# The order in which SyncE stores keys and queries and loads the last context, at the passage into cross attention

## The reference

```
x = x + attn1(layernorm(x))                      # one head, causal
q = (layernorm(x) @ Wq.T + bq), k = (ctx @ Wk.T + bk), v = (ctx @ Wv.T + bv)   # 16 heads of 8
scores = q k^T / sqrt(8), masked with -1e9; p = softmax(scores)
x = x + (p v) @ Wo.T + bo
x = x + ffn(layernorm(x))                        # quantised, 384 hidden
```

## Time and profile before

| | |
|---|---|
| median of 3 runs | 327.62 us (327.48 to 327.71) |
| the profiled execution | 325.96 us |
| its span, first to last instruction | 324.2 us |
| granted TensorE clock, mean | 0.994 |

### The profile page before, as it was taken

The page is one execution under the profiler, slowest core; times in us unless marked ns, Lnnn a source line. Parts: engine busy times, 40 slices in busy tenths (PEclk is TensorE's granted clock), DMA queues, the critical chain, the costliest instruction groups (busy, mean ns, idle before and its releaser), DMA issues.

```text
span 324.2 us, 10009 instructions
## 1 busy us (share of the span) xinstructions
PE 300.0 (93%) x3765; PEld 206.9 (64%) x3765; DVE 271.4 (84%) x653; ACT 255.3 (79%) x470; POOL 193.0 (60%) x340
## 2 busy tenths in 40 slices
PE   6999999997999999999999999899978689699996
PEld 5787877786656666666666666844323244359996
DVE  5489988787889989999999975877789996899764
ACT  3578888985889998989999987797797758994930
POOL 3679999981338796967749578200077773784000
PEclk9999999999999999999999999999997999999999
DMA  6951366642202566400000000000000000000134
GB/s 166 286 135 35 100 196 193 207 127 92 68 3 82 171 186 185 140 4 4 4 3 4 5 2 2 3 0 0 0 0 0 1 3 0 0 0 3 41 96 124
DMA packets 23754, 21.65 MB, mean 67 GB/s; under 512 B 3577, under 2 KB 21530, under 8 KB 23706
## 3 DMA queue, kind: packets, MB, share of 16 engines
q1 hardware_dynamic: 22170, 20.73, 21.3%
q10 hardware_dynamic: 1536, 0.28, 0.5%
HBM read 14.70 MB, written 6.30 MB: 65 GB/s over the span
## 4 chain that ended last, share of the span: by engine, by line
PE 51%; DVE 21%; ACT 9%; POOL 8%; issue 8%; DMA 2%; SPq 1%; POOLq 0%; ACTq 0%; DVEq 0%
DVE nm L1632 8%; PE banks L1016 8%; PE banks L1086 7%; DVE mxs L1860 6%; PE banks L786 5%; PE banks L730 5%; PE banks L660 4%; PE banks L621 4%; PE banks L653 3%; ACT ng L1393 2%; PE banks L808 2%; POOL rstd L391 2%; PE banks L723 2%; PE banks L672 2%; DVE mxs L1744 2%
## 5 line engine op out<-in xcount | busy, mean ns | idle before, releaser
L1632 DVE TENSOR_REDUCE nm<-banks 128x4 f32<-128x512 f32 x128 | 81.6, 680 | 6.5 <-PE banks L730 6.1
L1287 ACT ACTIVATE PT<-banks,bmask,vmask 128x1024 f32<-128x1024 f32 x64 | 76.8, 1202 | 0.1
L1016 PE MATMUL banks<-X3T,upT 128*128 128x512 f32 x96 | 45.9, 620 | 9.9 <-DVE mxs L1860 7.4
L590 POOL TENSOR_TENSOR G<-ng,sq 128x1536 int32<-128x1536 int32 (+3 forms) x10 | 27.9, 2795 | 36.4 <-DVE sq L1891 36.4
L1860 DVE TENSOR_REDUCE mxs<-G 128x1 f32<-128x1536 int32 (+5 forms) x32 | 42.4, 1345 | 4.2 <-ACT G L1354 3.8
L730 PE MATMUL banks<-kd,qd 32*128 32x128 f16 x512 | 39.3, 217 | 4.9 <-DVE nm L1632 2.5
L786 PE MATMUL banks<-PT,VP 128*32 128x128 f32 x1024 | 41.2, 279 | 0.5 <-ACT PT L1287 0.5
L1016 PEld LDWEIGHTS banks<-X3T,upT 128*128 128x128 f32 x96 | 17.7, 196 | 33.8 <-issue 16.3
L730 PEld LDWEIGHTS banks<-kd,qd 32*128 32x128 f16 x512 | 23.8, 92 | 22.4 <-DVE nm L1632 10.5
L1127 ACT ACTIVATE h<-X,shift,rstd 128x128 f32<-128x128 f32 x64 | 26.3, 483 | 7.3 <-POOL shift L436 7.3
L786 PEld LDWEIGHTS banks<-PT,VP 128*32 128x32 f32 x1024 | 24.1, 109 | 11.6 <-ACT PT L1287 5.3
(11 more groups left out here) (200 smaller groups left out, 729.2 us busy)
## 6 DMA issues: line engine op xcount, KB each, us to landing
kd<-k_dram SPq DMA_DIRECT2D x32, 128.0 KB, 2.7
qd<-q_dram SPq DMA_DIRECT2D x32, 128.0 KB, 2.7
ctxg<-in_ctx_dram SPq DMA_DIRECT2D x8, 256.0 KB, 3.1
out_dram<-y SPq DMA_DIRECT2D x7, 256.0 KB, 2.3
X<-in_x_dram SPq DMA_DIRECT2D x3, 512.0 KB, 7.1
X3T<-m_dram SPq DMA_DIRECT2D x1, 896.0 KB, 6.0
k_dram<-khi SPq DMA_DIRECT2D x7, 128.0 KB, 1.7
k_dram<-klo SPq DMA_DIRECT2D x7, 128.0 KB, 1.9
```

What stands on the lines that cost most here:

```text
L590: nc.gpsimd.tensor_tensor(GI[:, c], ng[:, u, part], sq[:, u, part], ALU.mult).then_inc(S["b_t"], 1)
L1016: m = pe.matmul(bank(2 + FC * (g % 2) + k), w[:, k * P:k * P + P], grp(X3T, g), start=True, stop=True)
L1287: act.activation(PT[:, a, :], bank(2 + 2 * a, 2), ACT.Exp, bias=bmask[:, n:n + 1], scale=vmask[:, n:n + 1]).then_inc(S["t_exp"], 1)
L1632: V.tensor_reduce(nm[:, n % 2, c:c + NSET], bank(u).rearrange("p (h m) -> p h m", m=P), AX.X, ALU.max, negate=True).then_inc(S["t_max"], 1)
```

## The change

For groups 0 to 3 nothing changes in SyncE's order. From group 4 on it is written out: keys 4, queries 4, keys 5, context 7, keys 6, queries 5, queries 6, keys 7, queries 7. Before it was keys 4, context 7, queries 4, keys 5, queries 5, keys 6, queries 6, keys 7, queries 7. Each step keeps its own waits. The condition in the loop, `0 < g`, selects groups 1 to 3 as `0 < g < NG // 2` did. No other engine's code is touched.

```
--- before.py
+++ after.py
@@ -350,13 +350,22 @@
 
             next_context(0)
             next_context(1)
-            for g in range(NG):
+            for g in range(NG - 4):
                 store_k(g)
                 next_context(g + 2)
                 store_q(g)
-                if 0 < g < NG // 2:
+                if 0 < g:
                     load_k(g - 1)
                     load_q(g - 1)
+            store_k(NG - 4)
+            store_q(NG - 4)
+            store_k(NG - 3)
+            next_context(NG - 2)
+            store_k(NG - 2)
+            store_q(NG - 3)
+            store_q(NG - 2)
+            store_k(NG - 1)
+            store_q(NG - 1)
             for g in range(NG // 2 - 1, NG):
                 load_k(g)
                 load_q(g)
```

## The result

The changed kernel took 323.65 us (median, 323.5 to 324.11), the kernel before 327.55 us (326.1 to 327.71) with the runs beside it: a ratio of 0.9898, 95% interval 0.9859 to 0.9936. The forecast was 325.5 (325.0 to 326.8): the sign was right, the size too small. The profiled execution took 323.5 us, against 325.96 of the one that the prediction read.

A forecast was written before the change was run, and what follows sets the result against it. The prediction took the late landing of keys 5, which held ScalarE's keys 6 and left TensorE idle before the first scores, as the bound; 327.62 - 2.14, all other terms 0, gave 325.5 us (325.0 to 326.8).

The forecast's parts named there:

- Steps 1 and 3: SyncE issues queries 4 at about 70.04, gaining nothing; ScalarE's high half of keys 6 starts at 75.32, gaining 2.14 us.
- step 2: SyncE issues keys 5 ahead of the context, 1.61 us earlier; they land about 74.5, between 73.8 and 75.8.
- Step 4: Around cross attention's entry, the rest follows the shift; nothing takes the wait's place: cost 0, bounds 0 to 0.3 us.
- Step 5: Last context load, issued 0.85 us later, lands at 75.4 before `pick_context(7)` at 78.35: 2.9 us of cover, cost 0.
- rival C: Last context lands too late for TensorE's `pick_context(7)`; 329.5 us at a 10 us landing; chance 0.07 with anything else slower.
- The rule of the Trainium skill: Context's signal comes only after earlier stores' writes, 75.8 with the slow landing, still under 78.35; the sum stays 2.14.
- Step 6: SyncE issues keys 6 ahead of queries 5, some nine microseconds earlier; nobody waits for that landing: cost and gain 0.
- the last: The sum for the whole kernel: 2.14 us taken off the shown runs' median of 327.62, giving 325.5.
- the price of the gap: TensorE's idle wait before cross attention's first scores: removing it gains 2.14 us, bounds 1.6 and 2.16.

The follow-up runs named there:

- ctx_last: Changed kernel's order with the last context load one step further back, behind keys 6: 328.06 us, ratio to the kernel before 1.0056.
- keys6_only: Kernel before with only keys 6 moved ahead of queries 5, context still ahead of queries 4 and keys 5: 326.18 us, ratio 0.9994.
- keys5_only: Kernel before with keys 5 ahead of the last context and queries 4 behind it: 323.46 us.
- stores_only: Kernel before with queries 4 and keys 5 ahead of the last context, keys 6 still behind queries 5: 323.49 us, ratio 0.9906.
- own_keys6: Kernel before, same SyncE order, with a buffer of their own for keys 6: 323.72 us.
- before_look2: Kernel before, unchanged, another execution for its trace: 327.6 us.
- before_look3: Kernel before, unchanged, another execution for its trace: 325.5 us.
- before_look1: Kernel before, unchanged, another execution for its trace: 325.67 us.
- q4_look2: Kernel before with queries 4 ahead of the last context and keys 5 behind it, second further execution for its trace: 325.98 us.
- again_after: Changed kernel, unedited, run again beside the kernel before: 323.74 us.
- q4_look1: Kernel before with queries 4 ahead of the last context and keys 5 behind it, another execution for its trace: 323.75 us.
- after: The changed kernel itself, against the kernel before: 323.65 us, ratio 0.9898.
- cold_start: Changed kernel without TensorE's five idle products at the start: 324.44 us.

## Why the prediction was right in its mechanism and wrong in its size

Steps 1 and 3 held to a few hundredths of a microsecond. With the execution's 0.32 us taken off, the forecast times were: queries 4 at 69.7 (69.70), keys 5 at 71.1 (71.11), khi of group 6 at 75.00 (75.00, released by `keys2(6)`), first scores at 76.32 (76.32). In step 2 the low keys went out at 71.47 where 71.6 was forecast; it took their landing at some 2.6 us, and it was 1.9. Step 4 held: the shift is 2.47 us at 250 us, and no other wait came up. Step 5 held, with 2.6 us of cover for the context where 2.9 were forecast; `ctx_last` shows what rival C would have cost, and that its price had been set too low. The rule of the Trainium skill on semaphores and earlier writes ("DMA: Bandwidth & Descriptors", section "Queues, rings and completion order"), which the prediction weighed, is not contradicted: the context's signal came at 75.5, after the stores' 73.4. Step 6 held in its price: keys 6 went out at 77.02, 0.4 us later than forecast, and `keys6_only` measures their place as nothing within 1 us.

The step that failed is the last, "the median of the runs shown is 327.62, and 327.62 - 2.14 = 325.5". It carried the 1.66 us between the median and the profiled execution over to the changed kernel as if it were a constant. It wasn't: 325.96 was an execution without a clock drop behind the gap, and the three that made the median were of a longer kind. The changed kernel has 323.65 in the median and 323.5 under the profiler, next to the 325.96 - 2.14 = 323.8 that the prediction had worked out and not used. The term of the sum that was mis-sized is the price of the gap. Idle, it cost 2.14 us in the trace read; over many executions it costs 326.8 - 323.65 = 3.2 us in the median. Of this its own length is about 2: among the executions with a mean clock of 1.000 the medians are 325.53 (23, gap idle), 325.76 (13, gap filled) and 323.52 us (14, no gap). The rest lies in the executions of the gap orders with a lower mean clock, and the drop behind the gap is one kind of them. Filling the gap takes 0.7 us off the median of all executions, 326.8 to 326.1, but with 24 executions that figure is loose: drawing them again at random puts it between 0.15 and 1.2. The gap itself varies too: 1.85, 2.15, 2.16, 2.17, 2.30 and 2.43 us in six traces of gap orders, 2.18 in the mean. What is left of the 3.2 us is not split up further here. The remaining 0.7 of the first 3.9 us lie in the few executions of the first comparison, whose interval (0.9859 to 0.9936) holds the 0.990 of the pooled medians.

Not shown: that those first three executions of before, at 327.5 to 327.7, were of the kind with the drop behind the gap; no trace of them exists. They can also have had the late clock at the start.

No version here beats the changed kernel beyond the spread: `keys5_only`, `stores_only` and `own_keys6` equal it.

## What to carry to other kernels

A store that frees the only buffer should be issued when its data is ready, ahead of a load that has microseconds of cover; look for the transfer queue's own waits in front of stores that were ready long ago. Price an idle gap on TensorE as more than its length: behind it the clock may fall, in a part of the executions, and one profiled execution can be of the other part. Where the profiled execution lies clear of the median, don't carry the difference over as a constant: ask which event makes it, and whether the change removes that too.

## What the runs showed of the hardware

- After a gap of 2.3 us on TensorE (`before_look2`) the granted clock was at 0.50, the lower level, from about 79.4 to 82.8 us; after gaps of 2.15 and 2.17 in `before_look3` and `before_look1` it stayed at 1.00. After 2.37 (`q4_look2`) and 2.43 us (`keys6_only`) it stayed as well, after 2.55 us (`ctx_last`) it fell. So the gap's length alone does not decide it here.
- The same clock drop near 245 us, in the feed-forward block, cost nothing: before had it from 245.0 to 248.4 and the changed kernel's profiled execution had not, and the shift between them is 2.46 to 2.47 us ahead of it and behind.
- At the start products of 128x128 can run at half their later rate (1.91 us per eight against 1.05) while a row of the profile reads 1.00 for the granted clock, because the first clock record of that trace, a rise, comes only at 17.2 us (`again_after`).
- Two executions of one kernel saw the same 128 KB store, issued behind a 256 KB load, land after 2.6 and 5.0 us (`q4_look1`, `q4_look2`); with only other stores ahead it took 1.9 (`after`). The issue of such a store took SyncE 0.43 us, and once 1.81 (`cold_start`).
